# Opening of a two-layer transformer kernel reordered, its FP4 passes spread over the first slots

## Chip, cores and metric

The kernel runs on one core of a Trainium2 chip. Its time is the device time of one execution in microseconds; all times below are microseconds unless ns is written. TensorE is PE, VectorE DVE, ScalarE ACT, GpSimd POOL, and SyncE, which issues the DMAs, SP.

## What is computed

Two sequences (batches) of 2048 tokens of width 128 go through two transformer layers. Each layer modulates its normalised input by vectors that come from a small conditioning vector `c`. Layer 0 has causal attention with rotary position tables and an FFN whose inputs and weights are quantised to FP4 in blocks of 16; layer 1 has attention through one combined matrix and a mixture of experts.

```
mod = silu(c) @ wmod;  sa, ca, ga, sb, cb, gb = six chunks of mod   # ga, gb kept 0.25 away from zero
h = layernorm(x) * (1 + ca) + sa
x = x + ga * attention(h)          # layer 0: softmax(rot(h Wq) rot(h Wk)^T / sqrt(128)) (h Wv)
h = layernorm(x) * (1 + cb) + sb
x = x + gb * ffn(h)                # layer 0: fp4(silu(fp4(h) fp4(w_gate)^T) * (fp4(h) fp4(w_up)^T)) fp4(w_down)^T
fp4(v): per block of 16, scale = max|v| / 6; round v / scale to the grid 0, .5, 1, 1.5, 2, 3, 4, 6; times scale
```

## The kernel before

All Python loops are unrolled; five engines each have their own stream of instructions, in the order in which the code writes them, and semaphores tie the streams together. An engine that waits for one semaphore holds up everything written behind it.

A batch is 16 tiles of 128 tokens; four tiles are a group. After an opening, the work of a batch runs in 32 slots: slot s finishes tile s of layer 0's attention (slots 0 to 15) and of layer 1's (16 to 31). In slot s PE first transposes inputs that are due (`input_turns`), then makes the scores of tile s+1, then projections for later groups, transposes tile s's probabilities and multiplies them with the values. DVE takes row maxima, rotates keys and queries of later groups, normalises the groups to come and finishes the tile; ACT takes exponentials and copies out of PSUM; POOL adds rotation sums, makes low parts and does the FP4 rounding of activations. FFN work lags by six slots (`FFN_LAG`), so the FFN weights are first read in slot 6 and `w_down` in slot 8. Group 2 is normalised on DVE in slot 1 and turned on PE in slot 2; group 3 in slots 3 and 4. ACT normalises the first FFN group in slot 4; POOL modulates it, DVE quantises it and POOL rounds it, all in slot 4 of their streams.

The opening before slot 0 (batch 0 only):
- SP issues the loads one after another: `c`, both `wmod`, `wq`, `wk`, `wv`, `gate_w`, half of batch 0's `x`, the FP4 weights (five loads, `w_down` last), the first rotation tables, the rest.
- PE turns `c`, makes nine columns of the modulation, the rows of the modulation, turns `wq`, `wk`, `wv`, turns the first normalised group, projects keys, keeps itself busy with 46 products (`keep_clock`, L659) until the keys are rotated, projects queries, turns the FP4 weights, then projects values (L725) and makes the first score product.
- DVE normalises group 0 (L1323), does the FP4 scaling of all 1120 columns of weights in one go (L1359 to L1365), normalises group 1, rotates keys and queries (L1333 to L1338), takes the modulation rows, forms layer 1's gate (L1296 to L1300, L1379), and takes the first maximum (L1387).
- POOL rounds the FP4 weights in three passes over 1120 columns (L528 to L532: add, subtract, multiply by the scale). ACT scales `w_down` by its gate (L1052) and copies the turned weights out of PSUM (L1055 to L1060).

## Time and profile before

| | |
|---|---|
| time, median of 3 runs (lowest, highest) | 708.12 (707.89, 708.60) |
| profiled execution's own span, first to last instruction | 705.9 |
| PE busy, share of the span | 633.8, 90% |
| DVE busy, share | 476.2, 67% |
| ACT busy, share | 340.6, 48% |
| POOL busy, share | 239.6, 34% |

The span is one execution on the chip; time and span differ by what lies around the first and the last instruction. Busy shares are means over stages: the opening, which ends near 39, has PE idle in many places, while the slots behind it keep PE busy nearly throughout. In a timeline row the first number is the start, the second the time until the last instruction of that row has ended, and in square brackets stands how long the engine had been idle before and what ended it.

### The profile page before, as it was taken

To read this page: it belongs to the slowest core of one execution; us is meant where nothing else is said; L and a number is where in the kernel's file an instruction comes from. 1 tells how busy PE (TensorE), PEld (TensorE's weight loads), DVE (VectorE), ACT (ScalarE), POOL (GpSimd) and SP (SyncE) were. 2 spreads that over 40 slices of the span, in tenths; PEclk is the share of its full clock that TensorE was granted. 3 is DMA by queue.
4 is the path that set the end of the run, shared out by engine and by line. 5 is a ranking of instruction groups with operands and counts; after the bars stand their busy time and mean duration, and the time that the engine had idled before them with its cause. 6 is when DMAs were issued, how large, how long until landed. Compare 5 with 4: busy or idle time off the path is not lost.

```text
span 705.9 us, 11080 instructions
## 1 busy us (share of the span) xinstructions
PE 633.8 (90%) x3839; PEld 487.1 (69%) x3839; DVE 476.2 (67%) x1270; ACT 340.6 (48%) x701; POOL 239.6 (34%) x320
## 2 busy tenths in 40 slices
PE   5799899988779899998899999869889998998996
PEld 4366687877556778775678777746768875676774
DVE  5965589786687557626569886688555527766665
ACT  1133464565535464433455465444555544454553
POOL 3424756462754211004557464484310002000000
PEclk9989999999999999999999999999999999999999
DMA  8200000000000000000000000100000000001011
GB/s 272 61 1 1 2 1 1 1 1 1 1 0 1 3 0 1 1 2 1 1 0 1 2 0 1 37 22 1 0 1 1 1 1 1 1 15 31 15 31 30
DMA packets 12174, 9.65 MB, mean 14 GB/s; under 512 B 1804, under 2 KB 10840, under 8 KB 12120
## 3 DMA queue, kind: packets, MB, share of 16 engines
q1 hardware_dynamic: 12120, 8.95, 4.2%
q8 instruction: 31, 0.51, 0.3%
q14 instruction: 23, 0.19, 0.1%
HBM read 6.84 MB, written 2.10 MB: 13 GB/s over the span
## 4 chain that ended last, share of the span: by engine, by line
PE 62%; DVE 21%; ACT 8%; issue 5%; POOL 3%; DMA 1%; SPq 0%; ACTq 0%; POOLq 0%; DVEq 0%
PE ps L840 13%; PE ps L705 10%; PE ps L818 8%; PE ps L990 4%; PE ps L992 4%; PE ps L991 4%; PE ps L664 4%; PE ps L863 2%; PE ps L864 2%; PE ps L725 2%; ACT xn L1108 2%; PE ps L659 2%; PE ps L879 2%; DVE row_max L1441 2%; POOL rstd L518 2%
## 5 line engine op out<-in xcount | busy, mean ns | idle before, releaser
L1172 ACT ACTIVATE probsT<-ps 128x512 f32<-128x512 f32 (+3 forms) x160 | 85.2, 533 | 158.4 <-PE ps L818 158.4
L840 PE MATMUL ps<-v_sb,probsT 128*128 128x129 f32 (+1 forms) x1124 | 151.4, 279 | 3.7 <-ACT probsT L1174 3.7
L840 PEld LDWEIGHTS ps<-v_sb,probsT 128*128 128x128 f32 (+1 forms) x1124 | 137.6, 191 | 8.8 <-ACT probsT L1174 5.5
L1441 DVE TENSOR_REDUCE row_max<-ps 128x1 f32<-128x512 f32 (+2 forms) x144 | 87.4, 619 | 51.2 <-PE ps L713 26.5
L818 PE MATMUL ps<-ident,probs 128*128 128x128 f32 (+1 forms) x562 | 90.2, 276 | 15.7 <-ACT hT L1100 7.8
L1146 ACT ACTIVATE probs<-ps,neg_max 128x512 f32<-128x512 f32 (+7 forms) x158 | 93.0, 620 | 10.4 <-DVE neg_max L1448 8.2
L818 PEld LDWEIGHTS ps<-ident,probs 128*128 128x128 f32 (+1 forms) x562 | 63.1, 139 | 47.6 <-issue 44.0
L554 POOL TENSOR_TENSOR hq<-ha,hp 128x352 f32<-128x352 f32 x32 | 29.8, 932 | 108.2 <-DVE hp L1491 108.2
L705 PE MATMUL ps<-k_high,q_high 128*128 128x512 f32 (+5 forms) x100 | 42.5, 425 | 6.0 <-ACT probs L1146 6.0
L659 PE MATMUL ps<-unpick,ident_b 128*128 128x512 bf16 x196 | 47.4, 383 | 0.3 <-ACT v_sb L1238 0.3
L517 POOL TENSOR_SCALAR minus_mean<-mv 128x4 f32<-128x4 f32 (+1 forms) x16 | 3.8, 237 | 121.5 <-DVE veps L1309 121.3
L1253 ACT ACTIVATE probs<-ps 128x512 f32<-128x512 f32 x40 | 24.0, 599 | 43.3 <-PE ps L992 43.3
L1463 DVE RECIPROCAL rsum<-ps 128x1 f32<-128x1 f32 x64 | 10.5, 164 | 48.6 <-PE ps L840 48.2
L1673 DVE TENSOR_TENSOR probs<-probs,ps 128x512 f32<-128x512 f32 x40 | 27.4, 686 | 19.9 <-ACT probs L1253 19.4
L990 PE MATMUL ps<-q_high,h_high 128*128 128x512 f32 x80 | 38.2, 478 | 1.6 <-DVE probs L1673 1.5
L1505 DVE SCALAR_TENSOR_TENSOR silu_g<-silu_g,ps 128x352 f32<-128x352 f32 x32 | 16.5, 515 | 30.6 <-ACT silu_g L1154 30.6
L705 PE MATMUL ps<-h_high,q_high 128*128 128x512 f32 (+2 forms) x80 | 35.9, 449 | 0.0
L863 PE MATMUL ps<-w_guT,xqT 128*128 128x352 f32 x64 | 25.3, 478 | 11.0 <-DVE q_low L1538 8.8
L705 PE MATMUL ps<-k_high,q_low 128*128 128x512 f32 (+5 forms) x100 | 34.9, 349 | 0.0
L705 PE MATMUL ps<-k_low,q_high 128*128 128x512 f32 (+5 forms) x100 | 34.9, 349 | 0.0
L879 PE MATMUL ps<-w_dg,hqT 128*128 128x128 f32 (+1 forms) x192 | 28.1, 282 | 4.5 <-ACT hqT L1159 4.5
L992 PE MATMUL ps<-q_high,h_low 128*128 128x512 f32 x80 | 31.6, 395 | 0.0
(245 smaller groups left out, 1390.0 us busy)
## 6 DMA issues: line engine op xcount, KB each, us to landing
out<-x_sb SPq DMA_DIRECT2D x8, 256.0 KB, 2.3
x_sb<-in_L_attn_x SPq DMA_DIRECT2D x2, 512.0 KB, 5.2
hT_all<-in_L_wmod SPq DMA_DIRECT2D x2, 384.0 KB
rope_cos<-table_cos SPq DMA_DIRECT2D x1, 768.0 KB, 6.3
rope_sin<-table_sin SPq DMA_DIRECT2D x1, 768.0 KB, 7.8
rope_cos<-table_cos SPq DMA_DIRECT2D x1, 256.0 KB, 3.4
rope_sin<-table_sin SPq DMA_DIRECT2D x1, 256.0 KB, 5.0
moe_raw<-in_L_ffn_expert_gate_w SPq DMA_DIRECT2D x1, 256.0 KB, 2.7
```

Source lines behind the costliest of these rows:

```text
L554: pool.tensor_tensor(hq[:, n % 2, :], ha[:], hp[:], ALU.add).then_inc(hq_step, 1)
L659: pe.matmul(bank(free_bank), ident_b[:], unpick[:].rearrange("p q n -> p (q n)"), start=True, stop=True)
L705: mm = pe.matmul(ps[:, cols], q_parts[q][:, tile], keys[k][:, cols], start=(n == 0), stop=(stop and n == len(passes) - 1))
L818: mm = pe.transpose(bank(TURN, k * P, (k + 1) * P, size), probs[:, s % 2, j * P:j * P + size], ident[:])
L840: mm = pe.matmul(bank(OUT_AT, 0, V_W), probsT[0:size, n % 4, k * P:(k + 1) * P], v_sb[0:size, j, :], start=(c == 0 and k == 0), stop=(c == ...
L863: pe.matmul(bank(GATE, 0, INNER), lhs, w_guT[:, 0:INNER], start=True, stop=True)
L879: mm = pe.matmul(bank(OUT_AT, DOWN.start, DOWN.stop), hqT[0:size, k * P:(k + 1) * P], w_dg[0:size, bass.ds(b, 1), k, :].rearrange("p a n - ...
L990: pe.matmul(dst, weights[0], high, start=start, stop=False)
L992: return pe.matmul(dst, weights[1], high, start=False, stop=stop)
L1146: act.activation(probs[:, s % 2, start:start + width], ps[:, start:start + width], ACT.Exp, bias=neg_max[:, s % 2:s % 2 + 1]).then_inc(exp ...
L1172: ins = act.activation(probsT[:, n % 4, 0:full], bank(TURN, 0, full), ACT.Copy)
L1441: ins = dve.tensor_reduce(dst, ps[:, start:start + width], AX.X, ALU.max, negate=single)
```

## The change

The opening is written in another order, and the FP4 work on the weights is cut in three pieces (`g`, `u`, `d` for `w_gate`, `w_up`, `w_down`).

- SP loads first the two columns of `wmod` that the first normalised group needs, four tiles of `x`, `wq` and `wk`; the FP4 weights follow; then the first tables, the next four tiles, the rest of `wmod`, `wv`, `gate_w`, and the other loads. Each has a semaphore of its own.
- POOL makes the identity mask first. PE turns `wq` and `wk` and makes two columns before anything else, projects keys and queries back to back (queries into banks 1 and 2), makes the other seven columns and the first score product, and only then turns `wv`, makes the modulation rows and projects values.
- DVE does the FP4 reduction ahead of the first normalisation and the FP4 scaling behind it; rotations and the first maximum go ahead of the rest of the modulation and of the last two FP4 instructions. Layer 1's gate goes from the opening to the end of slot 2 (`layer1_gate`).
- POOL's three passes run per piece at the end of its slots 1, 2 and 4 (`fp4_round`), PE's transposes in slots 3, 5, 6 and 7 (`turn_fp4`), ACT's copies in the same slots (`copy_fp4`), and ACT's scaling of `w_down` by its gate in slot 5 (`gate_fp4`), where it waits for all nine passes. FP4 scratch lies in the last columns of `probs`, which the early slots do not use.

The diff, cut to what the steps below need:

```diff
+        FP4_BANK = (2, 2, 3, 3)
+        FP4_ROUND_AT = {1: "g", 2: "u", 4: "d"}
+        FP4_TURN_AT = {3: 0, 5: 1, 6: 2, 7: 3}
...
-            for l, w in enumerate((wmod0, wmod1)):
-                sp.dma_start(wmod_sb[:, l, :], w).then_inc(c_loaded, 16)
-            for name, w in (("wq", wq), ("wk", wk), ("wv", wv)):
-                sp.dma_start(raw[:, RAW_AT[name], :], w).then_inc(attn_w_loaded, 16)
-            sp.dma_start(raw[0:EXPERTS, RAW_AT["gate_w"], :], gate_w).then_inc(attn_w_loaded, 16)
...
-            load_x(0, 0, TILES // 2, x_first_loaded)
+            sp.dma_start(wmod_sb[:, 0, 0:2 * P], wmod0[:, 0:2 * P]).then_inc(wmod_first_loaded, 16)
+            load_x(0, 0, GROUP, x_first_loaded)
+            for name, w in (("wq", wq), ("wk", wk)):
+                sp.dma_start(raw[:, RAW_AT[name], :], w).then_inc(attn_w_loaded, 16)
...
-            load_x(0, TILES // 2, TILES // 2, x_loaded)
+            load_x(0, GROUP, GROUP, x_second_loaded)
+            sp.dma_start(wmod_sb[:, 0, 2 * P:], wmod0[:, 2 * P:]).then_inc(wmod_loaded, 16)
+            sp.dma_start(wmod_sb[:, 1, :], wmod1).then_inc(wmod_loaded, 16)
+            sp.dma_start(raw[:, RAW_AT["wv"], :], wv).then_inc(wv_loaded, 16)
+            sp.dma_start(raw[0:EXPERTS, RAW_AT["gate_w"], :], gate_w).then_inc(wv_loaded, 16)
+            load_rope(BANK, SEQ, rope_loaded)
+            load_x(0, TILES // 2, TILES // 2, x_rest_loaded)
...
-            load_rope(BANK, SEQ, rope_loaded)
...
-            pool.wait_ge(fp4_scaled, 1)
-            pool.tensor_tensor(fp4_q, fp4_q, fp4_abs, ALU.add).then_inc(fp4_rounded, 1)
-            pool.wait_ge(fp4_rounded, 1)
-            pool.tensor_tensor(fp4_q, fp4_q, fp4_abs, ALU.subtract).then_inc(fp4_rounded, 1)
-            pool.wait_ge(fp4_rounded, 2)
-            pool.tensor_tensor(blocks(fp4_q), blocks(fp4_q), fp4_wide(1), ALU.mult).then_inc(fp4_rounded, 1)
+            def fp4_round(name):
+                n = "gud".index(name)
+                a = fp4_at[name]
+                z = a + (INNER if name == "d" else K_TILES * P)
+                q, m = fp4_q[:, a:z], fp4_abs[:, a:z]
+                scales = fp4_s[:, 1, a // BLOCK:z // BLOCK].unsqueeze(2).to_broadcast([P, (z - a) // BLOCK, BLOCK])
+                pool.wait_ge(fp4_scaled, 1)
+                pool.tensor_tensor(q, q, m, ALU.add).then_inc(fp4_rounded, 1)
+                pool.wait_ge(fp4_rounded, 3 * n + 1)
+                pool.tensor_tensor(q, q, m, ALU.subtract).then_inc(fp4_rounded, 1)
+                pool.wait_ge(fp4_rounded, 3 * n + 2)
+                pool.tensor_tensor(blocks(q), blocks(q), scales, ALU.mult).then_inc(fp4_rounded, 1)
             for b in range(BATCH):
...
+                    if b == 0 and s in FP4_ROUND_AT:
+                        fp4_round(FP4_ROUND_AT[s])
...
+            pe.transpose(bank(OUT_AT, 0, P), raw[:, RAW_AT["wq"], :], ident[:])
+            pe.transpose(bank(OUT_AT, P, 2 * P), raw[:, RAW_AT["wk"], :], ident[:]).then_inc(setup_pe, 1)
+            pe.wait_ge(setup_act, 1)
+            pe.wait_ge(wmod_first_loaded, 16)
+            mod_columns((0, 1))
+            pe.wait_ge(consts, 5)
+            keep_clock(0, 8)
+            pe.wait_ge(xn0_ready, 1)
+            pe.wait_ge(setup_act, 2)
+            turn_normed(0)
+            pe.wait_ge(copied, 1)
+            project_0(0, 0)
+            project_0(0, 1, FIRST_Q_BANKS)
+            pe.wait_ge(wmod_loaded, 32)
+            mod_columns(range(2, len(COLUMNS)))
+            keep_clock(0, 12)
+            pe.wait_ge(q_ready, 2)
+            score_products(0, 0)
+            pe.wait_ge(setup_dve, 2)
+            pe.wait_ge(wv_loaded, 32)
...
+            pe.wait_ge(setup_act, 3)
+            project_v_of(0, 0, wv_g)
...
+                    if b == 0 and n == 0:
+                        pe.wait_ge(fp4_ready, 2)
...
+                def turn_fp4(n):
+                    if n < BATCH:
+                        pe.wait_ge(fp4_rounded, 3 * (n + 1))
+                    else:
+                        pe.wait_ge(fp4_gated, n - BATCH + 1)
+                    if n % 2:
+                        pe.wait_ge(fp4_ready, n)
+                    for k, src in enumerate(FP4_T[n]):
+                        mm = pe.transpose(bank(FP4_BANK[n], k * P, k * P + src.shape[0], src.shape[1]), src,
+                                          ident[0:src.shape[0], 0:src.shape[0]])
+                    mm.then_inc(fp4_turned, 1)
...
                     for key in input_turns(b, s):
                         turn_group(key)
+                    if b == 0 and s == GROUP - 1:
...
+                    if b == 0 and s in FP4_TURN_AT:
+                        turn_fp4(FP4_TURN_AT[s])
...
+                           ACT.Copy).then_inc(setup_act, 1)
+            def copy_fp4(n):
+                act.wait_ge(fp4_turned, n + 1)
+                src = bank(FP4_BANK[n])
+                if n < 2:
+                    act.activation(w_guT[:, n * INNER:(n + 1) * INNER], src[:, 0:INNER], ACT.Copy).then_inc(fp4_ready, 1)
+                    return
+                src = src.rearrange("p (k n) -> p k n", n=P)
+                act.activation(w_dg[:, n - 2, 0:K_TILES - 1, :], src[:, 0:K_TILES - 1, :], ACT.Copy)
+                act.activation(w_dg[0:K_SIZE[-1], n - 2, K_TILES - 1, :], src[0:K_SIZE[-1], K_TILES - 1, :],
+                               ACT.Copy).then_inc(fp4_ready, 1)
+            def gate_fp4():
+                act.wait_ge(fp4_rounded, 9)
+                for b in range(BATCH):
+                    act.activation(fp4_d[:, b, :], fp4_q[:, fp4_at["d"]:], ACT.Copy,
+                                   scale=mod_col[:, b, GB0:GB0 + 1]).then_inc(fp4_gated, 1)
...
+                    if b == 0 and s in FP4_TURN_AT:
+                        copy_fp4(FP4_TURN_AT[s])
+                        if FP4_TURN_AT[s] == 1:
+                            gate_fp4()
...
-            dve.wait_ge(layer1_w_loaded, 48)
-            link(dve.tensor_tensor(ov_g[:], ov_raw[:].unsqueeze(1).to_broadcast([P, BATCH, P]), ga1_row[:], ALU.mult))
...
+            dve.wait_ge(x_rest_loaded, 16)
+            def layer1_gate():
+                at_least_quarter(ga1_row[:], ga1_row[:], "p (b n) -> p b n", (qa, qp))
+                dve.wait_ge(layer1_w_loaded, 48)
+                link(dve.tensor_tensor(ov_g[:], ov_raw[:].unsqueeze(1).to_broadcast([P, BATCH, P]), ga1_row[:], ALU.mult))
+                dve.wait_ge(x_loaded, 16)
             for b in range(BATCH):
...
+                    if b == 0 and s == 2:
+                        layer1_gate()
```

How the order moves, at three places. The number in `L...` is a line of the respective file.

DVE in the opening before, from the first FP4 instruction to the first rotation's end; `probs` holds the scaled weights here, `hT_all` the raw ones:

```order
L1359 TENSOR_REDUCE fp_s<-hT_all 128x70 [waits fp4_w_loaded]
L1360 TENSOR_SCALAR fp_s<-fp_s 128x70 [waits dve_step]
L1361 RECIPROCAL fp_s<-fp_s 128x70 [waits dve_step]
L1362 SCALAR_TENSOR_TENSOR probs<-hT_all,fp_s 128x1120 [waits dve_step]
L1364 TENSOR_SCALAR hT_all<-probs 128x1120 [waits dve_step]
L1365 TENSOR_SCALAR hT_all<-hT_all 128x1120 [waits dve_step]
L1323 TENSOR_SCALAR xn<-x_sb,mv,rstd 128x128 [waits rstd_ready_first]
L1323 TENSOR_SCALAR xn<-x_sb,mv,rstd 128x128 x3
L1333 TENSOR_TENSOR rope_t<-ps,rope_cos 128x512 [waits proj_ready,rope_first_loaded]
L1333 TENSOR_TENSOR rope_t<-ps,rope_sin 128x512 [waits proj_ready]
```

DVE in the opening of the changed kernel, from the FP4 reduction to the first rotation:

```order
L1403 TENSOR_REDUCE fp_s<-hT_all 128x70 [waits fp4_w_loaded,zeroed]
L1406 COPY mod_col<-ps 128x2 [waits setup_pe,dve_step]
L1407 TENSOR_SCALAR mod_col<-ps 128x2 [waits dve_step]
L1375 TENSOR_SCALAR xn<-x_sb,mv,rstd 128x128 [waits rstd_ready_first,dve_step]
L1375 TENSOR_SCALAR xn<-x_sb,mv,rstd 128x128 x3
L1409 TENSOR_SCALAR fp_s<-fp_s 128x70
L1410 RECIPROCAL fp_s<-fp_s 128x70 [waits dve_step]
L1411 SCALAR_TENSOR_TENSOR probs<-hT_all,fp_s 128x1120 [waits dve_step]
L1368 BN_STATS bn<-x_sb 128x6 [waits x_second_loaded,xn0_ready,dve_step]
L1368 BN_STATS bn<-x_sb 128x6 x3
```

The reduction has gone ahead of group 0's normalisation, and group 1's normalisation, which stood behind the FP4 work, has gone behind the first maximum.

ACT around the end of slot 5 before, from the last copies of tile 5's probabilities to the value copy of slot 6:

```order
L1172 ACTIVATE probsT<-ps 128x256 [waits pv_done,turned]
L1174 ACTIVATE probsT<-ps 1x128
L1181 ACTIVATE k_high<-rope_t 128x512 [waits rope_summed]
L1146 ACTIVATE probs<-ps,neg_max 128x512 [waits turned,max_ready]
L1146 ACTIVATE probs<-ps,neg_max 128x385
L1091 ACTIVATE xqT<-ps 128x128 [waits turned]
L1068 ACTIVATE v_sb<-ps 128x4x128 [waits v_proj_ready]
```

ACT at the same place in the changed kernel:

```order
L1226 ACTIVATE probsT<-ps 128x256 [waits pv_done,turned]
L1228 ACTIVATE probsT<-ps 1x128
L1103 ACTIVATE w_guT<-ps 128x352 [waits fp4_turned]
L1114 ACTIVATE probs<-probs,mod_col 128x352 [waits fp4_rounded]
L1114 ACTIVATE probs<-probs,mod_col 128x352
L1235 ACTIVATE k_high<-rope_t 128x512 [waits rope_summed]
L1200 ACTIVATE probs<-ps,neg_max 128x512 [waits turned,max_ready]
L1200 ACTIVATE probs<-ps,neg_max 128x385
L1145 ACTIVATE xqT<-ps 128x128 [waits turned]
```

One copy of a turned weight and the two scalings of `w_down`, with their wait for POOL, now stand between slot 5's copies and slot 6's exponentials.

POOL at the end of slot 4 and the start of slot 5 in the changed kernel (before, the last row followed directly on the multiplication by `qs`):

```order
L593 TENSOR_TENSOR xq<-qa,qp 128x384
L595 TENSOR_TENSOR xq<-xq,qp 128x384 [waits xq_step]
L599 TENSOR_TENSOR xq<-xq,qs 128x384 [waits xq_step]
L552 TENSOR_TENSOR probs<-probs,hT_all 128x352 [waits fp4_scaled]
L554 TENSOR_TENSOR probs<-probs,hT_all 128x352 [waits fp4_rounded]
L556 TENSOR_TENSOR probs<-probs,fp_s 128x352 [waits fp4_rounded]
L606 TENSOR_TENSOR rope_t<-rope_t 128x512 [waits roped]
```

Piece `d` has come in behind the rounding of the FFN's input and ahead of slot 5's rotation sum.

## Rows read from the trace of the kernel before

**Rows 1.** The page, part 1: busy time and share of the span, with instructions.

```profile
PE 633.8 (90%) x3839; PEld 487.1 (69%) x3839; DVE 476.2 (67%) x1270; ACT 340.6 (48%) x701; POOL 239.6 (34%) x320
```

**Rows 2.** Timeline of DVE in the opening: start, duration, line, operation.

```profile
10.20 0.17 DVE L1344 COPY mod_col<-ps 128x12 f32<-128x12 f32 x1 [0.18 <-PE ps L640]
12.00 0.48 DVE L1350 TENSOR_SCALAR wv_s<-raw,mod_col 128x128 f32<-128x128 f32 x2
12.39 1.11 DVE L1323 TENSOR_SCALAR xn<-x_sb,mv,rstd 128x128 f32<-128x128 f32 x4
14.94 1.31 DVE L1359 TENSOR_REDUCE fp_s<-hT_all 128x70 f32<-128x1120 f32 x1
17.74 1.33 DVE L1362 SCALAR_TENSOR_TENSOR probs<-hT_all,fp_s 128x1120 f32<-128x1120 f32 x1
20.54 7.64 DVE L1323 TENSOR_SCALAR xn<-x_sb,mv,rstd 128x128 f32<-128x128 f32 x4
28.09 0.68 DVE L1333 TENSOR_TENSOR rope_t<-ps,rope_cos 128x512 f32<-128x512 f32 x1
33.70 0.69 DVE L1338 TENSOR_TENSOR q_low<-rope_t,q_high 128x512 fp32r<-128x512 f32 x1
37.52 0.42 DVE L1379 TENSOR_TENSOR ov_g<-ov_raw,ga_row 128x256 f32<-128x256 f32 x1
```

**Rows 3.** Timeline of PE in the opening and slot 0.

```profile
10.02 2.05 PE L645 MATMUL ps<-hT_all,probsT 128*128 128x256 f32 x4
17.18 1.02 PE L664 MATMUL ps<-hT,wkrT 128*128 128x512 f32 x2
35.68 2.05 PE L725 MATMUL ps<-wv_g,hT 128*128 128x128 f32 x8 [1.66 <-ACT w_dg L1060]
42.65 1.02 PE L664 MATMUL ps<-hT,wkT 128*128 128x512 f32 x2
```

**Rows 4.** Timeline of SP's issue, and DMA issues with size and time to landing.

```profile
6.65 0.43 SPq L435 DMA_DIRECT2D hT_all<-in_L_ffn_w_down  x1
...
hT_all<-in_L_ffn_w_down SPq DMA_DIRECT2D x1, 176.0 KB, 4.6
out<-x_sb SPq DMA_DIRECT2D x8, 256.0 KB, 2.3
```

**Rows 5.** Timeline of slots 1 and 2: POOL, DVE, PE.

```profile
49.92 1.30 POOL L581 TENSOR_TENSOR rope_t<-rope_t 128x512 f32<-128x512 f32 x1 [0.93 <-DVE rope_t L1424]
...
49.75 2.06 DVE L1404 TENSOR_SCALAR xn<-x_sb,mv,rstd 128x128 f32<-128x128 f32 x4
...
51.87 0.66 PE L653 MATMUL ps<-ident,xn 128*128 128x128 f32 x4
```

**Rows 6.** One line's instructions each: durations in ns as min, median, max.

```profile
L1323 DVE TENSOR_SCALAR xn<-x_sb,mv,rstd x8: 337/341/2702, 12.4 to 25.9; 128x128 f32<-128x128 f32 x8
...
L1486 DVE SCALAR_TENSOR_TENSOR ha<-silu_g,qh x32: 524/525/1054, 90.9 to 502.7; 128x352 f32<-128x352 f32 x32
```

**Rows 7.** Timeline around slot 6's start (POOL, ACT, PE), and ACT's opening scalings.

```profile
83.76 0.84 POOL L574 TENSOR_TENSOR xq<-xq,qs 128x384 f32<-128x384 f32 x1
...
82.05 0.25 ACT L1174 ACTIVATE probsT<-ps 1x128 f32<-1x128 f32 x1
...
83.50 0.48 PE L705 MATMUL ps<-k_high,q_high 128*128 128x512 f32 x1
...
28.12 1.07 ACT L1052 ACTIVATE probs<-probs,mod_col 128x352 f32<-128x352 f32 x2 [11.96 <-POOL probs L532]
```

**Rows 8.** Timeline of slots 3 and 4: DVE, PE.

```profile
60.81 0.69 DVE L1441 TENSOR_REDUCE row_max<-ps 128x1 f32<-128x512 f32 x1
...
65.97 0.60 PE L653 MATMUL ps<-ident,xn 128*128 128x128 f32 x4
```

**Rows 9.** Timeline of PE, and PE in one stretch: length, busy, granted clock, DMA.

```profile
75.66 0.79 PE L705 MATMUL ps<-k_high,q_high 128*128 128x512 f32 x1 [1.61 <-ACT probs L1146]
...
76.00:79.00 3.00, 3.00 (x6) 0.50 0.00 0
```

More of the change, by code:

```diff
@@ L303, in build @@
         TURN, OUT_AT, GATE, UP = 4, 5, 6, 7
+        FIRST_Q_BANKS = (1, 2)
         DOWN = slice(2 * P, 3 * P)
@@ L735, in first_values_and_scores, with mod_columns @@
                 score_products(0, 0)
-            pe.wait_ge(setup_dve, 3)
-            first_values_and_scores(-1, 0)
+            def mod_columns(numbers):
+                for n in numbers:
+                    l, chunk = COLUMNS[n]
+                    mm = pe.matmul(bank(3, 2 * n, 2 * n + 2), wmod_sb[:, l, chunk * P:(chunk + 1) * P],
+                                   silu_c[:, 2 * l:2 * l + 2], start=True, stop=True)
+                mm.then_inc(setup_pe, 1)
+            pe.wait_ge(consts, 1)
@@ new lines, in _ @@
+            pe.wait_ge(setup_dve, 2)
+            pe.wait_ge(wv_loaded, 32)
+            for b in range(BATCH):
+                pe.transpose(bank(OUT_AT, b * P, (b + 1) * P), wv_s[:, b, :], ident[:])
+            pe.transpose(bank(OUT_AT, 2 * P, 2 * P + EXPERTS), raw[0:EXPERTS, RAW_AT["gate_w"], :],
+                         ident[0:EXPERTS, 0:EXPERTS]).then_inc(setup_pe, 1)
+            pe.wait_ge(roped, 4)
+            for b in range(BATCH):
+                pe.matmul(bank(1, b * 2 * P, (b + 1) * 2 * P), silu_cb[:, b, :], wmod_sb[:, 0, 3 * P:5 * P], start=True, stop=True)
@@ L740, in _ @@
+            for b in range(BATCH):
+                mm = pe.matmul(bank(2, b * P, (b + 1) * P), silu_cb[:, 2 + b, :], wmod_sb[:, 1, 2 * P:3 * P],
+                               start=True, stop=True)
+            mm.then_inc(setup_pe, 1)
+            pe.wait_ge(setup_act, 3)
+            project_v_of(0, 0, wv_g)
             for b in range(BATCH):
@@ new lines, in _ @@
+            at_least_quarter(mod_col[:, :, GB1:GB0 + 1], cols[:, :, GB1:GB0 + 1], "p (b n) -> p b n", (up_t, low_t))
+            for n in range(2 * BATCH):
+                last = dve.tensor_scalar(silu_cb[:, n, :], ones[:], silu_c[:, n:n + 1], None, ALU.mult)
+            last.then_inc(setup_dve, 1)
+            dve.wait_ge(wv_loaded, 16 * 2)
+            for b in range(BATCH):
+                last = dve.tensor_scalar(wv_s[:, b, :], raw[:, RAW_AT["wv"], :], mod_col[:, b, GA0:GA0 + 1], None,
+                                         ALU.mult)
@@ new lines, in _ @@
+            last.then_inc(setup_dve, 1)
+            first_maximum(-1)
+            first_normalise(-1, 0, 1)
+            link(dve.tensor_scalar(fp4_abs.bitcast(I32), fp4_q.bitcast(I32), EXPONENT, None, ALU.bitwise_and))
+            dve.tensor_scalar(fp4_abs, fp4_abs, 1.0, ROUND, ALU.max, ALU.mult).then_inc(fp4_scaled, 1)
+            dve.wait_ge(setup_pe, 6)
+            rows = bank(1).rearrange("p (b n) -> p b n", b=BATCH)
+            dve.tensor_copy(mod_row[:, :, 0, :], rows[:, :, 0:P])
+            dve.tensor_scalar(mod_row[:, :, 1, :], rows[:, :, P:2 * P], 1.0, None, ALU.add)
```

184 lines of the change are left out of this document (65 added, 119 removed).

## The prediction

> **What bounds the kernel now.** I read the page's engine shares first, then the opening in order of time, then what each engine waited for up to slot 8. PE is busy for 90% of the span [rows 1], so from slot 0 on nearly every microsecond that PE stands still is paid at the end. The opening is different: there PE waits for DVE, and DVE for POOL. DVE runs the FP4 passes over the weights (reduction at 14.94, scaling at 17.74), then four normalising instructions that take 7.64 instead of 1.11, then the two rotations from 28.09 to 34.39 [rows 2]. Only behind these come the value projection at 35.68 and the first key projection of slot 0 at 42.65 [rows 3]. The reader is to see that the stretch from 14.94 to 28.09 is FP4 work, or waiting for it, that slot 0 does not need. FFN weights are first read in slot 6.
>
> The time is 708.12, the profiled span 705.9; 2.2 lies around the span and I carry it over unchanged.
>
> **The opening, worked out.** T is the end of the first normalisation. In the new order it stands behind the reduction over all FP4 weights, so behind the load of w_down. That load was issued fourteenth, at 6.65, and landed 4.6 later. Now it is eleventh; at 0.43 an issue that is about 5.3 [rows 4]. Its landing is between 2.3 after issue (a 256 KB store with nothing ahead of it) and 4.6: between 7.6 and 9.9. Less is queued ahead of it, so I take 7.8, near the lower end. Then come the reduction 1.3, two short column operations 0.4 and the normalisation 1.1 [rows 2]: T = 10.6, bounds 10.4 to 12.7.
>
> Behind T, DVE does the scale, reciprocal and scaling (at most 1.5 between 16.25 and 17.74, and 1.33), then the second statistics (13.50 to 14.94, 1.4): about 4.0. The key projections need at most 4.7 (from 13.50 to 18.20), and 3.6 without PE's other work in that gap [rows 2, 3]; DVE sets the pace. The rotations take 6.3, to T+10.3. Then the columns of the modulation (10.20 to 12.00, 1.8), four copies at 0.24, two weight scalings 0.5, and the first maximum: T+13.9 [rows 2]. PE meanwhile fills with columns and clock-keeping products and has the score product ready before that. Behind it PE has three transposes (four took 0.66 in slot 2 [rows 5]) and the row products of the modulation. Their first half took 2.05 [rows 3] and the second has half the columns, so at most 3.1; I take 2.0, because at double clock it would be half. With the wait of PE for DVE's maximum and ACT's copy, the value projection thus starts at about T+16, 26.6. From there to slot 0's key projection took 6.97 (35.68 to 42.65) [rows 3], including the score products, which have now gone ahead, but the exponential now waits behind the value copy. I take 5.5, bounds 5 to 7. The key projection then starts at 32.1 instead of 42.65: a gain of 10.6. The bounds 8 and 12.5 come from T, the row products and the last stretch. The loads moved back on SP's queue cost nothing: the rest of wmod and wv are issued by about 9 and at 4.6 have landed by 14, PE wants the first of them behind both projections (about T+5.4, 16), and the remaining tables and x are asked for only ahead of slot 0. POOL's identity mask, moved to its front, lets PE begin with the weights that have landed; this is hidden ahead of T. POOL's three long passes fall away from the opening entirely, and with them the 6.5 that DVE's normalisation lost.
>
> **What comes back in the slots.** The work has not vanished.
>
> (a) Piece g, POOL, slot 1. It follows directly on POOL's rotation sum, which ran from 49.92 to 51.22 while DVE normalised group 2 from 49.75 to 51.81; PE's transpose of that group followed at 51.87 without slack [rows 5]. How a normalising instruction behaves beside POOL is seen at L1323: 337 ns alone, up to 2702 ns, and each long one ends with a POOL pass [rows 6]. A pass over 384 columns takes 1.0 (1.30 for 512 columns [rows 5], times 384/512) and the multiplying one 0.84 [rows 7]; three with their gaps are about 3.0. Two of DVE's four are still to come when piece g starts, and each waits out a pass of 1.0: +1.5, bounds 0 to 2.
>
> (b) Layer 1's gate on DVE (six instructions on 128x256, about 0.42 each, 2.5 free [rows 2]) is set ahead of the maximum at 60.81 [rows 8], while POOL starts piece u at about the same moment. PE's transpose at 65.97 waits for the normalisation that DVE has queued behind this maximum, its two rotations and a second maximum. Free of POOL, DVE loses 2.5, and some 0.8 of that fits into its own waits: +1.7. If the first two, with one input, each wait out a pass: +3.1. If the two-input ones wait too: +4.7. A two-input instruction on DVE took 1054 against 524 ns where POOL was in a pass [rows 6]. I take 4.0.
>
> The Trainium skill (SBUF — State Buffer, section "SBUF: two separate sides") says that the port pair which VectorE and GpSimd share is held for a whole instruction, also against a VectorE instruction with two SBUF inputs. By that rule (b) would be 4.7 and the time 0.7 above my forecast; if only one-input instructions waited it would be 0.9 below. The trace bears the rule out in the 1054 ns row.
>
> (c) The gate of w_down on ACT, slot 5. This is the largest term. ACT takes it after its last copy of slot 5 (ended 82.30) and ahead of the key rounding and the first exponential of slot 6; the score product at 83.50 waits for that exponential [rows 7]. It waits for piece d. POOL does piece d after the input's own FP4 passes, which end at 84.60, and 3.0 times 352/384 is 2.8: done at 87.4. The two scalings took 1.07: 88.5. ACT resumes 6.2 late, and PE stands at 83.50 behind it. Queued behind the wait on ACT are the rounding, both exponentials, the copy of xqT and the value copy, and PE waits for all of them. POOL's chain starts from ACT's own normalisation in slot 4, so the shifts before do not shorten it. +6.2, bounds 4.5 to 7.
>
> (d) Twelve transposes, two copies of w_guT and four of w_dg. Those of slots 3 and 5 lie inside the stalls (b) and (c). In slots 6 and 7, PE and ACT are both on the path for part of it: +0.8, bounds 0.3 to 2. The wait for the modulation rows in slot 3 costs nothing, since they are read before slot 0.
>
> (e) Clock. After an idle stretch PE ran from 76 to 79 at a granted 0.50, its 1.2 GHz level [rows 9], so about 3.4 of work cost 1.7 extra. Ahead of that PE had stood for 1.61 [rows 9]; stalls (b) and (c) are longer. One such loss each: +3.3, bounds 0 to 5.
>
> Sum: 1.5 + 4.0 + 6.2 + 0.8 + 3.3 = 15.8 back, 10.6 gained, +5.2: 713.3.
>
> **The rivals.**
> B, faster: the wait at ACT's gate is short. If POOL were through with piece d by the time ACT comes to it, (c) and its clock loss (7.9) go, and the result is 15.8 - 7.9 - 10.6 = -2.7: 705.4. It decides from where (c) with its clock loss falls below 2.7; with the clock holding that is piece d ending before about 83.9. For it speaks that POOL has idle gaps in slots 1 to 4; against it, that POOL takes its work in written order and piece d is written behind the input passes. Chance 0.18.
> C, about the same: the clock holds through both stalls (-3.3) and POOL and DVE hardly disturb each other in slot 3 (b at 1.7, -2.3): 10.2 - 10.6 = -0.4, 707.7. For it: PE is busy right up to both stalls, with clock-keeping products ahead of (b). Against it: the stall of 1.61 was enough once. Chance 0.20.
> D, slower still: the opening gains only 8, because w_down lands late and PE works at half clock: 715.9. Chance 0.07.
>
> **How the numbers follow.** The forecast, 713.3, has 0.55. What a measurement of this kernel can tell from no change is about 0.2%, 1.4. The forecast lies beyond that in nearly all of its width (0.52 slower, 0.03 same), D too; C splits 0.12 same, 0.07 faster, 0.01 slower; B (0.18) is faster. Slower 0.60, same 0.15, faster 0.25. The range takes in C, D and the nearer part of B: 705 to 717.5. With every term at its worst the sum is 20.7 - 8 = +12.7 (720.8), with every term at its best 6.5 - 12.5 = -6.0 (702.1); the terms are not tied to each other, and I leave both corners out.
>
> **What would show it.** In the changed profile: the value projection near 26.6 and slot 0's key projection near 31 to 33 (opening); DVE's normalising instructions of slot 1 near 1000 ns (a); the six gate instructions spread over more than 4 and PE idle ahead of the transposes of slot 4 (b); ACT idle by 4 to 5 ahead of its scaling of w_down, released by POOL, and PE idle by about 5 in slot 6 (c); granted clock of 0.50 behind these stalls (e). The forecast is wrong if ACT's gate finds piece d ready, or if the slots after 8 give back what slots 1 to 7 lost.

## The result and the profile after

The changed kernel takes 721.44 us, median of four runs (718.13 to 724.08), the kernel before 708.34 in runs beside it: ratio 1.0185, 95% interval 1.0151 to 1.0220. It is slower, as forecast, but by 13.1 us and not by 5.2, and outside the range. The profiled run is the longest of the four: 724.08, span 722.3, so 16.4 longer than the span before.

The page, part 1, and the clock line of part 2, beside [rows 1]. PE has 26 instructions fewer and is busy 4.7 longer; the other engines are busy within 1.2 of what they were.

```profile
PE 638.5 (88%) x3813; PEld 490.8 (68%) x3813; DVE 475.0 (66%) x1271; ACT 341.2 (47%) x701; POOL 240.6 (33%) x326
...
PEclk9988889999988999999999999998999999999999
```

The clock line of before, with slices of 18 us as well:

```profile
PEclk9989999999999999999999999999999999999999
```

With no more instructions than before, PE is busier because each took longer: its clock line is below 0.9 in slices 3 to 6, 12, 13 and 28, before in slice 3 alone.

Timeline of DVE in the opening, beside [rows 2]: the reduction over the FP4 weights, then the first normalisation, which ends at 11.04.

```profile
8.18 1.32 DVE L1403 TENSOR_REDUCE fp_s<-hT_all 128x70 f32<-128x1120 f32 x1 [1.96 <-DMA hT_all<-in_L_ffn_w_down]
...
9.93 1.11 DVE L1375 TENSOR_SCALAR xn<-x_sb,mv,rstd 128x128 f32<-128x128 f32 x4
```

Timeline of PE, beside [rows 3]: key projection, value projection, first score product of slot 1, key projection of slot 0.

```profile
12.62 2.02 PE L674 MATMUL ps<-hT,wkT 128*128 128x512 f32 x2 [0.87 <-ACT hT L1090]
...
27.22 1.91 PE L708 MATMUL ps<-wv_g,hT 128*128 128x128 f32 x8
...
31.50 0.38 PE L688 MATMUL ps<-k_high,q_high 128*128 128x256 f32 x1 [0.90 <-ACT probs L1129]
...
33.02 1.02 PE L674 MATMUL ps<-hT,wkT 128*128 128x512 f32 x2
```

Slot 0 begins 9.6 earlier (42.65 to 33.02). The first key projection ran at half clock (2.02 for two products that take 1.02 at 33.02), and so did most of the value projection (1.91), as it had before (2.05 [rows 3]).

Slots 1 to 6, beside [rows 5, 7, 8]: for each of the three new waits an instruction on POOL, one that it holds up (for the second wait two such pairs), and PE's wait.

```profile
41.55 0.99 POOL L552 TENSOR_TENSOR probs<-probs,hT_all 128x384 f32<-128x384 f32 x1
...
40.12 3.57 DVE L1465 TENSOR_SCALAR xn<-x_sb,mv,rstd 128x128 f32<-128x128 f32 x4
...
43.74 1.11 PE L663 MATMUL ps<-ident,xn 128*128 128x128 f32 x4 [1.44 <-DVE xn L1465]
...
56.21 1.00 POOL L554 TENSOR_TENSOR probs<-probs,hT_all 128x384 f32<-128x384 f32 x1
...
58.09 1.45 POOL L612 TENSOR_TENSOR k_low<-rope_t,k_high 128x512 fp32r<-128x512 f32 x1
...
56.31 1.04 DVE L1349 TENSOR_SCALAR qp<-ga_row 128x256 f32<-128x256 f32 x1
...
58.44 1.37 DVE L1351 SCALAR_TENSOR_TENSOR qp<-ga_row,qp 128x256 f32<-128x256 f32 x1
...
64.91 1.12 PE L663 MATMUL ps<-ident,xn 128*128 128x128 f32 x4 [3.90 <-DVE xn L1465]
...
87.98 0.79 POOL L556 TENSOR_TENSOR probs<-probs,fp_s 128x352 f32<-128x352 f32 x1
...
88.80 1.07 ACT L1114 ACTIVATE probs<-probs,mod_col 128x352 f32<-128x352 f32 x2 [3.95 <-POOL probs L556]
...
91.01 0.80 PE L688 MATMUL ps<-k_high,q_high 128*128 128x512 f32 x1 [5.51 <-ACT probs L1200]
```

Four stretches of the changed kernel: length, then busy time of PE, weight loads, DVE, ACT, POOL, then the granted clock (beside [rows 9]). The first three lie behind the three waits; the fourth lies far later, in slot 18.

```profile
44.00:50.00 6.00, 6.00 (x24) 4.63 (x24) 1.14 (x3) 1.89 (x3) 1.79 (x2) 0.50 0.00 0
...
65.00:71.00 6.00, 6.00 (x20) 4.54 (x21) 1.84 (x8) 1.38 (x2) 1.45 (x3) 0.52 0.01 3
...
91.00:95.00 4.00, 3.99 (x15) 3.47 (x15) 0.69 (x1) 1.19 (x3) 0.73 (x1) 0.55 0.00 0
...
211.00:218.00 7.00, 5.92 (x19) 4.42 (x20) 3.39 (x9) 1.58 (x4) 2.01 (x2) 0.50 0.00 0
```

The way to find where 16.4 us went is to take one PE instruction after the other and subtract its start after from its start before. This lead changes at few places:

| PE instruction | before | after | lead | lost since the line above to |
|---|---|---|---|---|
| slot 0, key projection | 42.65 | 33.02 | +9.6 | (opening's gain) |
| slot 2, transposes | 51.87 | 43.74 | +8.1 | 1.5, wait (a) |
| slot 2, first scores of slot 3 | 59.81 | 54.38 | +5.4 | 2.7, half clock |
| slot 4, transposes | 65.97 | 64.91 | +1.1 | 4.4, wait (b) |
| slot 5, first scores of slot 6 | 75.66 | 77.06 | -1.4 | 2.5, half clock |
| slot 6, input's first transpose | 83.42 | 85.17 | -1.8 | 0.4, slot 5's FP4 transposes, ahead of wait (c) |
| slot 6, first scores of slot 7 | 83.50 | 91.01 | -7.5 | 5.8, wait (c) |
| slot 7, input's transposes | 91.15 | 100.39 | -9.2 | 1.7: half clock 1.5, (d) 0.2 |
| first scores with a 0.79 wait | 98.34 | 109.32 | -11.0 | 1.7, (d) |
| slot 18, gate and up product | 200.35 | 211.45 | -11.1 | 0.1 |
| next gate and up product | 205.83 | 220.91 | -15.1 | 4.0, half clock |
| end of the span | 705.9 | 722.3 | -16.4 | 1.3, mostly slot 18 of the second batch |

At the fourth half-clock place the two kernels do the same work in the same order. One row of before and one of after, the gate product of slot 18, each with the wait ahead of it:

```profile
200.35 0.83 PE L863 MATMUL ps<-w_guT,xqT 128*128 128x352 f32 x2 [2.91 <-DVE q_low L1538]
```

```profile
211.45 1.51 PE L892 MATMUL ps<-w_guT,xqT 128*128 128x352 f32 x2 [2.92 <-DVE q_low L1599]
```

The same wait of 2.9, and behind it full clock in one run and half in the other (before, 200 to 207: granted 1.00). In the second batch the wait of slot 18 was followed by half clock in both kernels, for about 3 us before and for about 7 in the changed kernel.

### The profile page after: what moved, and what is told of

The parts are those of the page before. It is cut to its first block, busy times and chain, and to the rows that moved or that the text cites. A ratio compares the mean times of both kernels' runs of the same rounds, so it can differ in the third digit from the quotient of the medians.

```text
span 722.3 us, 11041 instructions
## 1 busy us (share of the span) xinstructions
PE 638.5 (88%) x3813; PEld 490.8 (68%) x3813; DVE 475.0 (66%) x1271; ACT 341.2 (47%) x701; POOL 240.6 (33%) x326
## 4 chain that ended last, share of the span: by engine, by line
PE 60%; DVE 21%; ACT 8%; POOL 5%; issue 5%; SPq 1%; DMA 0%; ACTq 0%; DVEq 0%; POOLq 0%
PE ps L867 12%; PE ps L688 10%; PE ps L845 7%; PE ps L1039 4%; PE ps L1041 4%; PE ps L1040 4%; PE ps L674 3%; PE ps L892 2%; PE ps L708 2%; PE ps L893 2%; PE ps L910 2%; ACT xn L1162 2%; POOL rstd L535 2%; DVE row_max L1502 2%; PE ps L669 1%
## 5 line engine op out<-in xcount | busy, mean ns | idle before, releaser
L867 PE MATMUL ps<-v_sb,probsT 128*128 128x129 f32 (+1 forms) x1124 | 153.1, 280 | 3.7 <-ACT probsT L1228 3.7
L1200 ACT ACTIVATE probs<-ps,neg_max 128x512 f32<-128x512 f32 (+7 forms) x158 | 93.1, 621 | 13.3 <-DVE neg_max L1509 11.1
L669 PE MATMUL ps<-unpick,ident_b 128*128 128x512 bf16 x170 | 44.5, 401 | 1.1 <-ACT v_sb L1296 1.1
L1524 DVE RECIPROCAL rsum<-ps 128x1 f32<-128x1 f32 x64 | 10.6, 165 | 49.7 <-PE ps L867 49.3
L688 PEld LDWEIGHTS ps<-k_high,q_high 128*128 128x128 f32 x100 | 19.6, 196 | 18.2 <-ACT probs L1200 14.6
```

The source lines that it names most:

```text
L669: pe.matmul(bank(free_bank), ident_b[:], unpick[:].rearrange("p q n -> p (q n)"), start=True, stop=True)
L688: mm = pe.matmul(ps[:, cols], q_parts[q][:, tile], keys[k][:, cols], start=(n == 0), stop=(stop and n == len(passes) - 1))
L867: mm = pe.matmul(bank(OUT_AT, 0, V_W), probsT[0:size, n % 4, k * P:(k + 1) * P], v_sb[0:size, j, :], start=(c == 0 and k == 0), stop=(c == ...
L1200: act.activation(probs[:, s % 2, start:start + width], ps[:, start:start + width], ACT.Exp, bias=neg_max[:, s % 2:s % 2 + 1]).then_inc(exp ...
```

## The experiments

Theory A: each of the three places costs its wait and the half clock behind it, and the waits have the causes that the prediction names. Rival B: the clock falls anyway. The ratios below are to the kernel before, run beside each; the changed kernel stands at 1.0185.

| run | us | ratio | 95% interval |
|---|---|---|---|
| piece d in slot 3 | 713.51 | 1.0078 | 1.0051 to 1.0105 |
| gate in slot 3 | 713.06 | 1.0082 | 1.0059 to 1.0105 |
| piece g ahead of slot 0 | 719.35 | 1.0146 | 1.0119 to 1.0174 |
| all three | 704.76 | 0.9949 | 0.9932 to 0.9965 |
| pieces g and u ahead | 714.53 | 1.0066 | 1.0040 to 1.0093 |
| the three waits fed | 716.47 | 1.0105 | 1.0075 to 1.0135 |
| slot 18 fed | 715.69 | 1.0099 | 1.0079 to 1.0119 |
| before, slot 18 fed | 705.88 | 0.9962 | 0.9949 to 0.9975 |
| FP4 work early | 702.10 | 0.9900 | 0.9875 to 0.9925 |
| and first exponential first | 698.68 | 0.9851 | 0.9830 to 0.9872 |
| and slot 18 fed | 696.23 | 0.9834 | 0.9816 to 0.9851 |
| and opening fed | 697.14 | 0.9849 | 0.9828 to 0.9869 |

**One wait taken away at a time.**

```diff
-        FP4_ROUND_AT = {1: "g", 2: "u", 4: "d"}
+        FP4_ROUND_AT = {1: "g", 2: "u", 3: "d"}
```

> The changed kernel with one number changed: the FP4 passes of piece d stand on POOL in slot 3 and not in slot 4, so that they end (about 71 us) long before ACT reaches the gating of w_down in slot 5. Theory A (the stall and the half clock behind it are both due to this wait): ACT's gating waits for PE's transposes only, PE's 5.51 us wait in front of the slot-7 scores at 91.01 us falls under 0.5, the 1.5 us of half clock behind it go too, and the time falls from 721.4 by about 7 us, to 714. Rival B (only the stall comes back, the clock falls anyway in the same stretch): by 5.5, to 716. Rival C (piece d in slot 3 runs beside DVE or ahead of POOL's statistics and modulations and costs what it saves): under 3 us, to 718.5 or above.

Measured: 7.9 less than the changed kernel. ACT no longer waits for POOL, but PE's wait does not vanish (ACT and PE, slots 5 and 6):

```profile
81.06 1.05 ACT L1114 ACTIVATE probs<-probs,mod_col 128x352 f32<-128x352 f32 x2
...
83.27 0.50 PE L688 MATMUL ps<-k_high,q_high 128*128 128x512 f32 x1 [1.45 <-ACT probs L1200]
```

5.51 has become 1.45: what remains is ACT's own copy, scaling and rounding ahead of the exponential, so 4.1 came from the wait for POOL. Theory A's "under 0.5" does not hold, and that its time came out is in part luck. In the profiled pair this place gave back the 4.1 and 0.3 of the half clock behind it. Much of the rest lies where the edit does nothing: in slot 2 the transposes stood behind the same wait of 1.44 and then ran at full clock, so that the 2.7 were not lost there, and in slot 18 half clock took 1.6 and not 4.0.

```profile
43.91 0.66 PE L663 MATMUL ps<-ident,xn 128*128 128x128 f32 x4 [1.44 <-DVE xn L1465]
```

PE still stood 1.45 ahead of the half clock that stayed, so between A and B this run does not decide; the run with the three waits fed does.

```diff
-                    if b == 0 and s == 2:
+                    if b == 0 and s == 3:
                         layer1_gate()
```

> The changed kernel with one number changed: the layer-1 gate (six operations on DVE) runs at the end of slot 3, behind the last normalisation of the opening, and not at the end of slot 2 in front of it. Theory A (stall plus clock): PE's 3.90 us wait for the normalised tiles at 64.91 us falls to 0.3 or less, the half clock from 65 to 71 us goes with it, and the time falls from 721.4 by 4.4 + 2.2 = 6.6 us, to 715. Rival B (stall alone): by 4.4, to 717. Rival C (the six operations only move the wait to the next row maximum and rotation of slot 4): the time stays within 1.5 us of 721.4.

Measured: 8.4 less. Behind the last normalisation the six operations cost PE nothing: the wait in slot 4 is 0.23. In the profiled pair 6.1 of the gain lie here, 3.7 of wait and 2.4 of half clock, close to theory A's 6.6; the remainder lies elsewhere. The first of the six, and PE's transposes:

```profile
61.19 0.29 DVE L1348 TENSOR_SCALAR qa<-ga_row 128x256 f32<-128x256 f32 x1
...
59.92 0.66 PE L663 MATMUL ps<-ident,xn 128*128 128x128 f32 x4 [0.23 <-DVE xn L1465]
```

```diff
-        FP4_ROUND_AT = {1: "g", 2: "u", 4: "d"}
+        FP4_ROUND_AT = {2: "u", 4: "d"}
...
+            fp4_round("g")
             for b in range(BATCH):
                 def modulate_1(g):
```

> The changed kernel with the FP4 passes of piece g ahead of slot 0 on POOL (from about 27.5 us, where POOL stood idle until 35.7) and not in slot 1 beside DVE's normalisation of 3.57 us. Theory A: the normalisation takes 2.06 us again as before, PE's wait of 1.44 us in slot 2 goes, and with it the half clock from 44 to 50 us: from 721.4 by 1.5 + 2.6 = 4.1 us, to 717.3. Rival B (the clock falls there without the wait too): by 1.5, to 720. Rival C: the passes run beside DVE's copies at 27.5 to 29 us, delay the first products, and nothing is won.

Measured: 2.1 less by the medians, 2.8 by the ratios, between A and B. The wait and its half clock are gone. The timeline has DVE's normalisation and PE's transposes without a wait, the stretch behind them a granted clock of 1.00:

```profile
40.55 2.05 DVE L1466 TENSOR_SCALAR xn<-x_sb,mv,rstd 128x128 f32<-128x128 f32 x4
...
42.66 0.66 PE L664 MATMUL ps<-ident,xn 128*128 128x128 f32 x4
```

```profile
43.00:49.00 6.00, 5.45 (x30) 3.24 (x28) 2.56 (x7) 2.27 (x4) 1.31 (x2) 1.00 0.00 0
```

> The three edits of the other runs together: piece g ahead of slot 0, piece d in slot 3, the layer-1 gate at the end of slot 3. Theory A (three places, each a stall with a half-clock stretch behind it, adding up): 721.4 - 7.3 - 6.6 - 4.1 = 703.4 us, under the kernel before by 5; runs lie as close together as those of the kernel before. Rival B (stalls alone, clock losses stay): 721.4 - 5.8 - 4.4 - 1.5 = 709.7 us, no faster than the kernel before. Rival C (the opening order itself is worth less than the 9.6 us by which slot 0 begins earlier, because the half clock follows it): 707 to 710 with no stall left in slots 2, 4 and 6.

Measured: 704.76, 16.7 less than the changed kernel, where the single runs add up to 18.4: the three places are nearly independent, and theory A's 703.4 is close. Against the kernel before that is 0.5% faster. The order of the opening is thus worth having; its price was the place that the FP4 work got. The runs do not lie as close together as those of before (701.57 to 707.14). By slot 5 this kernel leads the one before by 9.4, and 5.2 of it are lost between slots 6 and 8. The timeline of ACT and PE there, and the stretch behind (granted clock 0.62):

```profile
73.89 1.05 ACT L1115 ACTIVATE probs<-probs,mod_col 128x352 f32<-128x352 f32 x2
74.85 0.61 ACT L1236 ACTIVATE k_high<-rope_t 128x512 fp32r<-128x512 f32 x1
75.37 1.15 ACT L1201 ACTIVATE probs<-ps,neg_max 128x512 f32<-128x512 f32 x2
...
76.09 0.50 PE L689 MATMUL ps<-k_high,q_high 128*128 128x512 f32 x1 [1.45 <-ACT probs L1201]
```

```profile
76.00:80.00 4.00, 3.91 (x16) 3.48 (x17) 0.69 (x1) 1.63 (x5) 1.75 (x2) 0.62 0.00 0
```

**The gate's own length and what POOL adds.** Pieces g and u both stand ahead of slot 0 (`fp4_round("u")` behind `fp4_round("g")`), the gate stays in slot 2.

> The changed kernel with the FP4 passes of both pieces g and u ahead of slot 0 on POOL; the layer-1 gate stays at the end of slot 2 on DVE. It tells the gate's own length from what POOL beside it adds. Theory A (POOL's piece u beside the gate holds DVE up): the six operations take 2.2 us and not 5.27, PE's wait in slot 4 falls from 3.90 to 0.8 us, and against the run with piece g alone ahead (719.4) the time falls by 3.1 us and up to 2.2 us of half clock: 714 to 716.3. Rival B (the six operations are slow by themselves in this place): they keep 5 us, and the time stays at 719.

Measured: 4.8 less than with g alone ahead by the medians, 714.53 inside theory A's range. First and last of the six operations on DVE, and PE's wait:

```profile
50.97 1.27 DVE L1350 TENSOR_SCALAR qa<-ga_row 128x256 f32<-128x256 f32 x1
...
53.99 0.42 DVE L1452 TENSOR_TENSOR ov_g<-ov_raw,ga_row 128x256 f32<-128x256 f32 x1
...
58.58 0.85 PE L665 MATMUL ps<-ident,xn 128*128 128x128 f32 x4 [1.86 <-DVE xn L1467]
```

The six take 3.44 (50.97 to 54.41) instead of 5.44 (55.29 to 60.73); the first, at 1.27, lies beside another pass of POOL (the low half of the keys, 50.83 to 52.10). PE's wait falls from 3.90 to 1.86. So 2.0 of wait (b) is POOL's piece u at the gate, and 1.9 the gate's place ahead of the normalisation.

**The clock by itself.** The waits stay; PE gets products to do in them.

```diff
-WAITED_FOR = {**{("norm0", g): 3 for g in range(1, GROUPS)},
+WAITED_FOR = {**{("norm0", g): 3 for g in range(1, GROUPS)}, ("norm0", 2): 9, ("norm0", 3): 18,
...
+                    if b == 0 and s == 7 and c == 0:
+                        pe.wait_ge(roped, 4 * GROUPS)
+                        keep_clock(GATE, 23)
                     pe.wait_ge(exp_done, ...)
```

> The changed kernel with the three waits left as they are, but PE given products to do in them (whose results nobody reads): 6 more ahead of the slot-2 transposes, 15 more ahead of the slot-4 transposes, 23 ahead of the first slot-7 scores, each 0.24 us at full clock, so that they fill the waits of 1.44, 3.90 and 5.51 us without making them longer. Theory A (the half clock behind each wait follows from PE's standing still in it): the granted clock stays at full from 44 to 50, 65 to 71 and 91 to 95 us, and the time falls from 721.4 by 2.6 + 2.2 + 1.7 = 6.5 us, to 715. Rival B (the half clock comes from something else in this stretch, or the products only lengthen the waits): the time stays within 2 us of 721.4.

Measured: 5.0 less by the medians, 5.7 by the ratios. The timeline has PE's first instruction behind each wait, the stretches the granted clock in about the six us that follow:

```profile
43.23 0.66 PE L663 MATMUL ps<-ident,xn 128*128 128x128 f32 x4 [0.16 <-DVE xn L1468]
...
61.68 0.66 PE L663 MATMUL ps<-ident,xn 128*128 128x128 f32 x4 [0.65 <-DVE xn L1468]
...
85.35 0.50 PE L688 MATMUL ps<-k_high,q_high 128*128 128x512 f32 x1 [0.50 <-ACT probs L1203]
```

```profile
43.00:49.00 6.00, 5.71 (x32) 3.58 (x31) 2.53 (x7) 1.89 (x3) 2.19 (x3) 1.00 0.00 0
62.00:68.00 6.00, 5.85 (x35) 4.00 (x33) 3.12 (x11) 1.97 (x3) 1.98 (x4) 1.00 0.00 0
85.00:91.00 6.00, 5.31 (x33) 4.21 (x34) 1.72 (x4) 2.48 (x6) 1.08 (x1) 1.00 0.00 0
```

The waits still cost what they did (the lead falls by 4.4 at (b) and by 6.1 at (c), slot 5's FP4 transposes included); the half clock behind all three is gone. It follows from PE's standing still there.

```diff
                 def gate_up(n):
                     g, t = divmod(n, GROUP)
+                    if group_at(n + FFN_LAG, Q1_SLOT) == 1:
+                        keep_clock(3, 12)
```

> The changed kernel with 12 products (0.24 us each at full clock, results not read) ahead of the gate and up products of slot 18, where PE stands 2.9 us for DVE's low query half in every kernel here; behind that wait the changed kernel's trace has half clock at 211 to 218 us and 4 us of further loss, the trace of before has not. Theory A (the loss past slot 6 is half clock behind this same wait): the clock stays full there and the time falls from 721.4 by 3 to 5 us, to 717. Rival B (the half clock at 211 us hangs on something else, or comes at another wait instead): within 1.5 us of 721.4.

Measured: 5.8 less, above theory A's 3 to 5; the products stand in slot 18 of both batches. The timeline has PE's gate product in slot 18, the stretch the clock around it:

```profile
210.81 0.83 PE L894 MATMUL ps<-w_guT,xqT 128*128 128x352 f32 x2 [0.34 <-DVE q_low L1601]
```

```profile
209.00:216.00 7.00, 6.00 (x34) 3.90 (x33) 4.66 (x12) 1.96 (x5) 3.26 (x4) 1.00 0.00 0
```

> The kernel before with the same 12 products ahead of the gate and up products of slot 18, as a control: its trace has full clock behind this wait in the first batch and 0.91 from 460 to 480 us in the second. Theory A: 0.5 to 1.5 us are won, in the second batch alone, 707.5. Rival B: the products lengthen the wait or change nothing, 708.3 or more.

Measured: the control gained too, 2.2 by the medians, more than either theory had. Its trace shows slot 18 of both batches at full clock (460 to 500 granted 1.00, in before 0.96 over the same stretch). In the profiled pair 1.4 is won at slot 18 of the second batch, as theory A had it, so this wait was costing the kernel before as well. Another 1.7 is there ahead of slot 18 of the first batch, where the edit does nothing. It comes from the opening: the control's value projection ran at full clock and not at half as in [rows 3], and slot 0 began 1.9 earlier. The control's value projection and key projection of slot 0:

```profile
35.70 1.13 PE L725 MATMUL ps<-wv_g,hT 128*128 128x128 f32 x8 [1.66 <-ACT w_dg L1062]
...
40.72 1.02 PE L664 MATMUL ps<-hT,wkT 128*128 128x512 f32 x2
```

The same two in the changed kernel with slot 18 fed:

```profile
27.71 1.06 PE L708 MATMUL ps<-wv_g,hT 128*128 128x128 f32 x8
...
32.67 1.02 PE L674 MATMUL ps<-hT,wkT 128*128 128x512 f32 x2
```

With the value projection at full clock on both sides the new opening is ahead by 8.05, not by 9.6. How much of the 2.2 is due to the products stays open, and with it how much of the 5.8 is the changed kernel's own: 3.6 if all of the 2.2 is.

**A faster version.** FP4 work away from ACT's crowded slots, on top of the three edits:

```diff
+        FP4_ROUND_AT = {2: "d"}
+        FP4_TURN_AT = {1: 0, 2: 1, 4: 2, 5: 3}
+        FP4_BANK = (2, 2, 2, 2)
...
+            fp4_round("g")
+            fp4_round("u")
...
+                    if b == 0 and s == GROUP - 1:
+                        gate_fp4()
```

> On top of the edits that took the three waits away (704.8 us): piece u ahead of slot 0 as well, piece d at the end of slot 2, ACT's gating of w_down at the end of slot 3, the FP4 transposes with ACT's copies in slots 1, 2, 4, 5 and not in 3, 5, 6, 7. There PE still stood 1.45 us at the slot-7 scores behind ACT's gating, copy and rounding, then ran at half clock, and 5.2 us of the 9.4 us that slot 5 began earlier were gone by slot 8. Theory A (ACT's FP4 work of slots 5 to 7 is the cause): the lead of 9 us holds up to slot 8, and the time is 699 to 701 us. Rival B (these waits belong to the slots themselves, as the kernel before has them in other places, and the copies only move them): 703 to 705 us.

Measured: 702.10, 0.9900, between the theories in time. In the trace theory A holds in the main: the lead is 9.0 at the first scores of slot 6 and 7.8 at those of slot 7, where the wait is 0.60; it lasts to slot 18, where half clock takes 2.7. With the three edits alone, 4.2 were left by slot 8.

```profile
75.68 0.51 PE L690 MATMUL ps<-k_high,q_high 128*128 128x512 f32 x1 [0.60 <-ACT probs L1202]
```

```diff
-            put_v_at(0, 0)
             first_exp(-1)
+            put_v_at(0, 0)
```

> The run before with one more edit: ACT takes the first exponential, with the 1.28 us table load ahead of it, before the copy of the first values and not behind it; the maximum that it needs is there at 25 us, the values only at 29 us. Theory A: PE's wait of 0.90 to 1.28 us for that exponential ahead of the slot-1 scores (at 30.9 to 31.9 us) goes, and slot 0 and all behind it begin 0.9 us earlier. Rival B (another chain ends as late, the copied transposes of the second group): under 0.3 us.

Measured: 3.4 less where A had 0.9. The table load and the exponential now end long before the values, and PE's scores of slot 1 have no wait:

```profile
24.86 1.28 ACT L1131 ACT_TABLE_LOAD   x1
26.16 0.37 ACT L1131 ACTIVATE probs<-ps,neg_max 128x129 f32<-128x129 f32 x1
...
29.24 0.37 PE L690 MATMUL ps<-k_high,q_high 128*128 128x256 f32 x1
```

In the profiled runs 1.9 of it is there at the first scores of slot 1 (31.10 to 29.24). But 1.6 is there already at the value projection (27.68 to 26.09), ahead of the edit's place, behind key and query projections that ran at half clock in one run and not in the other; in this run the value projection then ran at half clock. The rest is mostly slot 18, at full clock in this run. How much of the 3.4 the edit itself is worth beyond 1.3, the wait that went, stays open.

> The fastest version so far (FP4 work early, first exponential ahead of the values; 0.985 of the kernel before) with the same 12 products in slot 18. Its profiled run had no half clock there in the first batch, 0.96 in the second. Theory A: 0.5 to 2 us are won in the median and the runs lie closer together, 0.983 of the kernel before. Rival B: no difference, 0.985.

Measured: 696.23, 0.9834; the runs lie within 2.0 (695.60 to 697.62). This is the fastest version by its median, 1.7% below the kernel before; its interval overlaps that of the version without these products (0.9830 to 0.9872).

> The run before with products in the opening too: 6 more ahead of the first normalised tiles' transposes (PE stands 0.4 to 1.5 us there) and 3 between them and the first key projection (0.87 us). In most traces here the key and query projections behind these two waits run at half clock from 13 to 19 us, in one they do not. Theory A: the projections run at full clock always, and 1 to 2 us are won: 0.981 of the kernel before. Rival B: DVE's rotations end as late by their own length, or the products make the transposes late: within 0.5 us of the run before.

Measured: 0.9849, no gain; rival B by the time. The profiled pair does not test theory A: the key and query projections ran at full clock in both (1.13 for the first two products in both), and DVE's opening is the same to 0.03 up to 25.7. What differs comes behind: the value projection ran at half clock here (1.91 against 1.28), and slot 0's key projection began 1.3 later (32.10 against 30.80). So what the clock of the key projections is worth stays open.

## Why the prediction was wrong in size

- **The opening, right in its order, 1.0 short, and that with luck.** 9.6 gained, 10.6 forecast. T was 11.04 and not 10.6 (w_down landed at 8.18, forecast 7.8); the value projection came at 27.22 (26.6), and from there 5.80 (5.5) to the key projection. The luck is that the forecast and the gain both count from 42.65 [rows 3], behind a value projection at half clock; in the two runs with slot 18 fed, where it ran at full clock, the gain is 8.05, at the lower bound of 8.
- **(a), right as a wait, 1.5, and incomplete.** The normalisation took 3.57 beside piece g and 2.05 without it. What followed was not counted: 2.7 of half clock behind PE's wait of 1.44. The prediction gave such a loss to (b) and (c) only, though its own row showed one behind a wait of 1.61 [rows 9].
- **(b), right: 4.4 against 4.0.** Four of the six operations took 0.99 to 1.37, three beside piece u and the fourth beside the pass behind it (the low half of the keys, 58.09 to 59.54). The two with two inputs among them (1.02, 1.37) waited as the others did, so the reading with 4.7 had the mechanism; the last two operations ran free. The Trainium skill (SBUF — State Buffer, section "SBUF: two separate sides") says that a VectorE instruction with two SBUF inputs contends with a GpSimd instruction that reads SBUF for the shared port pair too; the trace agrees: the same two took 0.42 and 0.43 away from POOL, in the run with pieces g and u ahead.
- **(c), right: 6.1 against 6.2,** with the 0.4 of slot 5's FP4 transposes, which lie inside this stall as forecast. Piece d in slot 3 took away 4.1 of PE's wait. The rest was ACT's own FP4 work, which sat under the wait for POOL and stood there when that was gone. Rival B fell because POOL takes its work in written order: piece d ended at 88.77.
- **(d), 2.0 against 0.8.** 0.2 is PE's transposes of slot 6 (the run with the waits fed loses as much there at full clock), 1.7 comes in slot 7 and at the scores behind it: ACT's copies in slots 6 and 7 stand ahead of an exponential that PE waits for.
- **(e) is the step that failed: 3.3 forecast with an upper bound of 5, 12.0 in the profiled run.** It counted one loss of 1.7 behind each of (b) and (c) and none elsewhere. Behind the three waits it was 2.7 + 2.5 + 1.5 = 6.7. Another 4.0 came in slot 18 and 1.3 later, where nothing was changed and nothing was counted. The median of 721.44 thus lies beyond even the corner with every term at its worst, 720.8. Feeding the three waits gave back 5.0 to 5.7, feeding slot 18 gave 5.8. If the two add up (by the ratios 5.7 and 6.1), which was not run, the changed kernel would be at 709.6, and the forecast without term (e) is 710.0.
- **The side was right, and rival C wrong:** C let the clock hold and put (b) at 1.7.

With the new terms the sum stands: 1.5 + 4.4 + 6.1 + 2.0 + 12.0 - 9.6 = 16.4, the growth of the profiled span. The median run lost 13.1. Of the four runs the longest has the lowest mean granted clock (0.967 at 724.08) and the shortest the highest (0.977 at 718.13).

The half clock in slot 18 is not peculiar to the changed kernel. Ten traces here have this wait of 2.9 in both batches without products in it. In 17 of these 20 places the granted clock fell to 0.5 within 2 us behind the wait, for about 3 to 9 us; in three it stayed at 1.00 for the next 8, and the first batch of the profiled run before is one of the three. So part of what the changed kernel seems to lose from slot 18 on is the luck of the run that it is compared with. What decides whether the clock falls behind this wait is not settled.

## What to carry to other kernels

Price a wait on PE as the wait and the half-clock stretch that may follow it, here 1.5 to 2.7 for each of the three and 4.0 in slot 18, and allow for such a loss at the waits that the change does not touch too. The length of the wait alone did not tell where: half clock followed 1.44 in slot 2 of the changed kernel and, in 17 of 20 places, 2.9 in slot 18, but not once in 28 places the 1.5 in slot 14. Compare more than one profiled run, since a stretch of half clock in the run before counts as a gain of the change. Work taken out of an opening goes where its engine, the engine beside it and the engine that needs the result all stand still: moving two of three FP4 pieces and one gate by a slot or two gave back 16.7 us here. Where a wait can't go, products that nobody reads kept the clock at every wait where these runs put them behind slot 0; in the kernel before that was worth 1.4 us in the trace.
